# Three edits to a four-layer transformer kernel on one Trainium2 core: first keys loaded during the layer's norm, four of sixteen heads scaled by ScalarE, the norm's root taken on columns and spread by TensorE

## The reference, cut to what matters

```python
x = x + tanh(g_xattn[l]) * xattn_l(layernorm(x), ctx)
x = x + tanh(g_ffn[l])   * ffn_l(layernorm(x))
```

```python
for i in range(6):
    q, k, v = split(shift_tokens(x) @ Wqkv[i])
    q, k = rope(l2norm(q) * qs), rope(l2norm(k) * ks)
    x = local_attention(q, k, v) @ Wo[i] + x
    t = shift_tokens(x)
    xn = (t - mean(t)) / sqrt(var(t) + 1e-5) * g + b
    a, gate = split(xn @ W1 + b1)
    x = (a * gelu(gate)) @ W2 + b2 + x
```

## Time and profile before

| what | value |
|---|---|
| profiled execution | 8037.15 us, span on the core 8035.4 us |
| three other runs | median 8040.48 us (8039.37 to 8040.94) |
| attention, layer 0: norm's first instruction to the first maximum | 160.50 to 207.03 us |
| local transformer, six layers | 5294 to 6711 us, 235.5 us each |
| of these 235.5 us: first rotation to last copied head | 5539.32 to 5614.27 us in the second layer |

### The profile page before, as it was taken

One profiled execution on the slowest core, in us unless ns is written; L12 is line 12 of the kernel. 1 busy time (PEld: TensorE's weight loads), 2 busy tenths in 40 slices (PEclk: granted clock), 3 DMA queues, 4 the chain that ended last, 5 costly groups with the idle time before them and its releaser, 6 DMA issues. The chain is left out here.

```text
span 8035.4 us, 123712 instructions
## 1 busy us (share of the span) xinstructions
PE 5948.6 (74%) x45093; PEld 1946.0 (24%) x45093; DVE 6533.6 (81%) x11562; ACT 5210.8 (65%) x8393; POOL 755.1 (9%) x394
## 2 busy tenths in 40 slices
PE   5699997499997455534555777767888875899987
PEld 2122222122222111101110111134444442222223
DVE  5999972699992899999997999966656665999934
ACT  3399995089997455424545999954555551699992
POOL 2000000000000000000000000054435540000000
PEclk8699999699998555555557999988989996899998
DMA  7100001300000000000002000000000002000001
GB/s 220 40 16 5 18 2 48 73 4 18 17 3 4 22 8 8 13 4 8 8 4 50 17 17 3 1 30 14 9 14 11 9 9 59 3 17 18 3 2 48
DMA packets 112345, 176.36 MB, mean 22 GB/s; under 512 B 14817, under 2 KB 94725, under 8 KB 106750
## 3 DMA queue, kind: packets, MB, share of 16 engines
q1 hardware_dynamic: 111774, 168.91, 8.3%
HBM read 125.66 MB, written 43.21 MB: 21 GB/s over the span
## 5 line engine op out<-in xcount | busy, mean ns | idle before, releaser
L1034 DVE TENSOR_REDUCE a_partial<-a_row 128x2 f32<-128x988 f32 x2496 | 2739.8, 1179 | 130.7 <-PE a_row L908 127.6
L999 ACT ACTIVATE a_prob<-a_score 128x512 f32<-128x512 f32 x4896 | 2649.4, 595 | 110.8 <-PE a_score L921 98.4
L934 PE MATMUL a_acc<-a_prob,a_v_all 128*9 128x256 f32 x19584 | 1526.1, 384 | 0.6 <-ACT a_prob L999 0.6
L517 ACT COPY m_rows<-m_score 128x1536 f32<-128x1536 f32 (+1 forms) x640 | 760.9, 1250 | 847.2 <-DVE m_edge L568 691.4
L908 PE MATMUL a_row<-a_kg,a_qn 54*128 54x494 bf16 x4992 | 1030.9, 410 | 272.1 <-DVE a_partial L1034 212.6
L576 DVE MAX8 m_cand<-m_rows 128x8 f32<-128x192 f32 x4352 | 1213.8, 332 | 13.6 <-ACT m_rows L517 13.6
L496 PE MATMUL m_score<-m_kb,m_qb 54*128 54x512 bf16 (+1 forms) x1664 | 766.3, 608 | 415.3 <-ACT m_rows L517 349.4
L921 PE MATMUL a_score<-a_qb,a_kg 54*128 54x512 bf16 x4896 | 939.4, 380 | 70.8 <-ACT a_prob L999 25.7
L798 DVE SCALAR_TENSOR_TENSOR a_prob<-a_score,a_prob 128x1024 f32<-128x1024 f32 x816 | 925.0, 1216 | 37.9 <-ACT a_prob L774 37.9
L774 ACT ACTIVATE a_prob<-a_score,a_lower 128x1024 f32<-128x1024 f32 x816 | 865.9, 1111 | 84.6 <-PE a_score L715 34.1
L908 PEld LDWEIGHTS a_row<-a_kg,a_qn 54*128 54x128 bf16 x4992 | 243.6, 94 | 1386.8 <-DVE a_partial L1034 1228.9
(11 more groups left out here) (305 smaller groups left out, 5692.5 us busy)
## 6 DMA issues: line engine op xcount, KB each, us to landing
kst<-kv_parts SPq DMA_DIRECT2D x48, 384.0 KB, 3.9
a_kg<-kst SPq DMA_DIRECT2D x60, 306.0 KB
vst<-kv_va SPq DMA_DIRECT2D x48, 288.0 KB, 4.1
e_cb<-comb SPq DMA_DIRECT2D x25, 512.0 KB
a_kg<-kst SPq DMA_DIRECT2D x60, 204.0 KB
a_v_all<-vst SPq DMA_DIRECT2D x3, 3672.0 KB
qst<-q_parts SPq DMA_DIRECT2D x24, 256.0 KB
a_kg<-kst SPq DMA_DIRECT2D x60, 102.0 KB
```

The lines of the kernel that those rows point to most:

```text
L517: act.copy(rows[i][:, c * CH:c * CH + n], score[(i * NCH + c) % 2][:, 0:n]).then_inc(copied, 1)
L934: last = pe.matmul(acc[32 * j:32 * j + VW, columns], v_all[:, k, u // NQC * G + j, :], prob[tile % PROBS][:, j // 2, j % 2, columns], star ...
L999: act.activation(prob[tile % PROBS][:, j // 2, j % 2, :], score[use % 3][:, :], ACT.Exp).then_inc(slot_out, 1)
L1034: dve.tensor_reduce(partial[:, u % 2, 2 * item:2 * item + 2, c], row[use % 2][:, :, 0:CW], AX, ALU.max).then_inc(reduced, 1)
```

## The change

**First keys.** For layers 0, 1 and 3 the stage allocates `first_keys` (which takes the place of the buffer `kg[0]`) and a semaphore `first_loaded`. `norm_transpose` gets a SyncE program that issues the eight DMAs of heads 0 and 1; `attend_with_max` issues only those of heads 2 and 3 at its start.

**Scaling.** GpSimd multiplies heads 0 to 11 (`LP = 12`); ScalarE multiplies heads 12 to 15 by four instructions of 128x64 per step, after the root and before `keep_heads`. The transposes of a step wait for both, and so does VectorE's inversion two steps later.

**Root on columns.** The variance now comes as columns: per half four matmuls with the squares as stationary operand and one column of `mean_ones` as moving operand. Root and reciprocal work on 128x4 values. Four matmuls per half with the broadcast column as stationary operand and the identity as moving operand spread it over all partitions again, and VectorE multiplies by that PSUM tile.

```diff
-def norm_transpose(nc, xs, ident, xT, tag):
+def norm_transpose(nc, xs, ident, xT, tag, first_loads=None):
...
+        if first_loads is not None:
+            @block.sync
+            def _(sp):
+                first_loads(sp)
...
+def load_first_keys(sp, first_keys, first_loaded, kst_l, kmask_l):
+
+    for j in range(2):
+        load_key_rows(sp, first_keys[64 * j:64 * j + ROWS, 0, :], kst_l[j], kmask_l, first_loaded)
...
-            load_keys(0)
+            load_keys(0, range(2, G))
...
             def turn_heads(layer, s):
                 n = layer * STEPS + s
                 pe.wait_ge(S["scaled"], n + 1)
+                pe.wait_ge(S["scaled_act"], n + 1)
...
-                    pe.matmul(bank[2 + half], mean_ones[:, :], f_sq[half], start=True,
-                              stop=True).then_inc(S["var_done"], 1)
+                    for i in range(HALF // P):
+                        last = pe.matmul(bank[4 + half][:, i:i + 1], f_sq[half][:, i * P:(i + 1) * P], mean_ones[:, 0:1],
+                                         start=True, stop=True)
+                    last.then_inc(S["var_done"], 1)
+                for half in range(2):
+                    pe.wait_ge(S["rstd_ready"], layer * 2 + (half + 1))
+                    for i in range(HALF // P):
+                        last = pe.matmul(bank[2 + half][:, i * P:(i + 1) * P],
+                                         rstd_cols[:, half, i:i + 1].to_broadcast([P, P]), ident[:, :], start=True,
+                                         stop=True)
+                    last.then_inc(S["spread"], 1)
...
+            def scale_rest(n):
+                act.wait_ge(S["rn_ready"], n + 1)
+                act.wait_ge(S["added"], n + 1)
+                for h in range(LP, LH):
+                    last = act.activation(t1[n % T1S][:, h, :], t1[n % T1S][:, h, :], ACT.Copy,
+                                          scale=rnorm[:, n % 2, h, :])
+                last.then_inc(S["scaled_act"], 1)
...
-                    act.activation(f_a[half], bank[2 + half], ACT.Sqrt, bias=eps[:, 0:1]).then_inc(S["std_ready"], 1)
+                    act.activation(std_cols[:, half, :], bank[4 + half][:, 0:HALF // P], ACT.Sqrt,
+                                   bias=eps[:, 0:1]).then_inc(S["std_ready"], 1)
...
-                pool.tensor_tensor(t1[n % T1S][:, :, :], t1[n % T1S][:, :, :],
-                                   rnorm[:, n % 2, :, :].to_broadcast([P, LH, LD]), ALU.mult).then_inc(S["scaled"], 1)
+                pool.tensor_tensor(t1[n % T1S][:, 0:LP, :], t1[n % T1S][:, 0:LP, :],
+                                   rnorm[:, n % 2, 0:LP, :].to_broadcast([P, LP, LD]), ALU.mult).then_inc(S["scaled"], 1)
...
-                    dve.reciprocal(f_b[half], f_a[half]).then_inc(S["rstd_ready"], 1)
-                    dve.wait_ge(S["rstd_ready"], layer * 2 + (half + 1))
-                    dve.tensor_tensor(f_x[half], f_r[half], f_b[half], ALU.mult).then_inc(S["xn_mul"], 1)
+                    dve.reciprocal(rstd_cols[:, half, :], std_cols[:, half, :]).then_inc(S["rstd_ready"], 1)
+                for half in range(2):
+                    dve.wait_ge(S["spread"], layer * 2 + (half + 1))
+                    dve.tensor_tensor(f_x[half], f_r[half], bank[2 + half], ALU.mult).then_inc(S["xn_mul"], 1)
```

More of the change, by code:

```diff
@@ L803, in _, with attend_with_max @@
             heads(UNITS - 1)
-def attend_with_max(nc, kst_l, kmask_l, vst_l, qst, ident, att, tag):
+def load_first_keys(sp, first_keys, first_loaded, kst_l, kmask_l):
+    for j in range(2):
+        load_key_rows(sp, first_keys[64 * j:64 * j + ROWS, 0, :], kst_l[j], kmask_l, first_loaded)
+def attend_with_max(nc, first_keys, first_loaded, kst_l, kmask_l, vst_l, qst, ident, att, tag):
     UNITS = NG * NQC
@@ L819, in attend_with_max @@
         m = Memory(nc, ctx, tag)
-        kg = [m.sb(f"kg{i}", [P, 2, KPAD], BF16) for i in range(2)]
+        kg = [first_keys, m.sb("kg1", [P, 2, KPAD], BF16)]
         qn = [m.sb(f"qn{i}", [P, 2, QC], BF16) for i in range(2)]
@@ L833, in attend_with_max @@
         qn_loaded = [m.sem(f"qn_loaded{i}") for i in range(2)]
-        kg_loaded = [[m.sem(f"kg_loaded{i}{pair}") for pair in range(2)] for i in range(2)]
+        kg_loaded = [[first_loaded, m.sem("kg_loaded01")], [m.sem(f"kg_loaded1{pair}") for pair in range(2)]]
         cleared, v_loaded = m.sem("cleared"), m.sem("v_loaded")
@@ L863, in _, with load_keys @@
         def _(sp):
-            def load_keys(g):
-                for j in range(G):
+            def load_keys(g, heads=range(G)):
+                for j in heads:
                     load_key_rows(sp, kg[g % 2][64 * (j % 2):64 * (j % 2) + ROWS, j // 2, :], kst_l[g * G + j], kmask_l,
@@ L1571, in local_transformer @@
     T1S = 4
+    LP = 12
     with ExitStack() as ctx:
@@ L1579, in local_transformer @@
         eps = m.sb("eps", [P, 1])
+        std_cols, rstd_cols = m.sb("std_cols", [P, 2, HALF // P]), m.sb("rstd_cols", [P, 2, HALF // P])
         mean_ones = m.sb("mean_ones", [P, P])
@@ L1600, in local_transformer @@
             "cleared", "setup", "loaded", "wqk", "wvo", "w12", "tables", "shifted",
-            "proj", "squared", "roped", "added", "summed_sq", "root", "inverted", "rn_ready", "scaled", "turned_qk", "kept_qk",
+            "proj", "squared", "roped", "added", "summed_sq", "root", "inverted", "rn_ready", "scaled", "scaled_act", "turned_qk", "kept_qk",
             "v_done", "v_kept", "sc_done", "maxed", "exped", "rs_ready", "rinv_ready", "normed", "turned", "pt_ready",
             "pv_done", "o_ready", "y_done", "z_ready", "mean_done", "xc_ready", "xsq_ready", "var_done", "std_ready",
-            "rstd_ready", "xn_mul", "xn_ready", "h_done", "gelu_ready", "hh_ready", "f_done")}
+            "rstd_ready", "spread", "xn_mul", "xn_ready", "h_done", "gelu_ready", "hh_ready", "f_done")}
         halves = lambda t: [t[:, :, :].rearrange("p h d -> p (h d)")[:, i * HALF:(i + 1) * HALF] for i in range(2)]
@@ L1815, in _ @@
                         root(n - 1)
+                    if 2 <= s < STEPS + 2:
+                        scale_rest(n - 2)
                     if s >= 3:
@@ L1931, in invert @@
                     dve.wait_ge(S["scaled"], n - 1)
+                    dve.wait_ge(S["scaled_act"], n - 1)
                 dve.reciprocal(bounded[:, n % 2, :, 0:1], norm[:, n % 2, :, :]).then_inc(S["inverted"], 1)
@@ L2052, in attention @@
                 top, att = s.sb("top", [P, H * NT]), s.sb("att", [P, NT, D])
-                norm_transpose(nc, xs, ident, xT, f"n{l}")
+                first_loads = None
+                if l != 2:
+                    first_keys = s.sb("first_keys", [P, 2, KPAD], BF16)
+                    first_loaded = s.sem("first_loaded")
+                    first_loads = lambda sp: load_first_keys(sp, first_keys, first_loaded, kst[l], kmask[l])
+                norm_transpose(nc, xs, ident, xT, f"n{l}", first_loads)
                 queries(nc, xT, a[f"wq{l}"], a[f"bq{l}"], float(score_scale[l]), qst, f"q{l}")
@@ L2059, in attention @@
                 else:
-                    attend_with_max(nc, kst[l], kmask[l], vst[l], qst, ident, att, f"a{l}")
+                    attend_with_max(nc, first_keys, first_loaded, kst[l], kmask[l], vst[l], qst, ident, att, f"a{l}")
                 project(nc, att, a[f"wo{l}"], a[f"bo{l}"], a["g_xattn"][l:l + 1], xs, ident, f"p{l}")
```

## The result

The changed kernel takes 7951.4 us (median of 4 runs, 7950.9 to 7955.7), the kernel before beside it 8040.7: ratio 0.9889, interval 0.9875 to 0.9903, 89 us less. The forecast was 7939. The profiled execution took 7955.7 us with a span of 7953.9, the longest of the four. From one attention's norm to the next, the changed kernel's trace is shorter by 10.9, 9.0 and 9.0 us in layers 0, 1 and 3, and by 52.6 us in layer 2, where the local transformer is.

A forecast was written before the change was run, and what follows sets the result against it. Bounds: key waits at attention starts, GpSimd's pace in stage 1 with VectorE close behind, and stage 3's chain at half clock. Gains 27 + 29 + 45 = 101 us from 8037.15 gave 7936, 7939 for the median; range 7908 to 7975.

The forecast's parts named there:

- First keys: Attention start, layers 0, 1, 3: queries 17.3 us earlier less 7.5 for late `q_w`, three times, less clearings: 27 us.
- Root on columns: Stage 3 of the local transformer: third weight block 7.6 us earlier in each of six layers, 45 us.
- The three places: Key waits at attention starts (58.1 us), GpSimd's 4.18 us step in stage 1, stage 3's chain with TensorE's clock at 0.50.
- what is taken off the keys' wait comes off the total: Attention: the 114 maxima behind the wait run back to back on VectorE and need no other late load.
- The rival in which `q_w` passes the keys: Attention start: DMA engines give the small load a turn, nothing is late; 22 us more gained, 7917; chance 0.07.
- The clearings: Three more semaphore clearings with a meeting of all engines, put at 0.7 us each.
- Scaling by ScalarE: Stage 1 of the local transformer: GpSimd's step becomes 3.72, VectorE's 3.85 is next; 4.9 us a layer, 29 in six.
- the 15 steps of 3.84 without a wait: Stage 1: 15 steps of 3.84 and 2.50 from first rotation to first addition reach the last addition 4.4 us earlier.
- This holds if the clock stays up. It should: Stage 3: condition of the 7.6 us a layer, TensorE keeping its full clock; called the least certain term.
- The rival for that case: Stage 3: the clock falls all the same; 2.5 us gained a layer, 15 in six, time 7969; chance 0.27.
- gaps of under 1 us are too short for a fall: Stage 3: the 5.59 us without work shrink to gaps under 1 us filled with small matmuls, so TensorE's clock should stay.
- Slower: Stage 1: ScalarE becomes the bound, deciding at 0.73 us a scaling; at 0.8 the time is about 8080; chance 0.03.

The follow-up runs named there:

- weights_first: Changed kernel with the queries' weight and bias loaded in the norm's block ahead of the key DMAs in layers 0, 1 and 3; 7932.4 us.
- clock_stage3: Changed kernel with filling matmuls on TensorE in stage 3 (12 before the means, 3 behind them, 3 behind the squares' sums); 7947.8 us.
- all_three: Changed kernel with weights ahead of keys (layer 2 too) and filling matmuls at stage 2's end and in stage 3, two more between the sums' halves; 7887.8 us.
- keys_only: Kernel before with only the first head pair's keys loaded from the norm on; 8008.8 us.
- scaling_only: Kernel before with only ScalarE scaling four of sixteen heads; 8019.1 us.
- root_only: Kernel before with only root and reciprocal on columns, spread by TensorE; 7994.6 us.
- pool8: Changed kernel with 8 heads scaled by GpSimd and eight by ScalarE; 7940.1 us.
- pool14: Changed kernel with 14 of 16 heads scaled by GpSimd and two by ScalarE; 7946.6 us.

## Why the prediction was right, and where its sizes were off

*What bounds.* The three places were read rightly: each edit alone gained in its own stage, more than measurement noise. One step did not hold in full, that what is taken off the keys' wait comes off the total: 28.9 of 34.0 us did.

*First keys*, forecast 27 us: measured 29 between the traces, 31 alone. That this is so near is in part two errors that cancel. The gain at the first key product was 11.4, 10.8 and 11.8 us instead of 9.8, since `q_w` lost 6.2, 6.6 and 5.3 instead of 7.5 and the queries arrived 3.0 us after their issue instead of 3.4; against these 4.6 us more than forecast stand the 4.5 lost before the last maxima. The rival in which `q_w` passes the keys is out; what it would have been worth, 19 us measured by weights_first, was there for moving two issues. The clearings: about 1.2 us for 2.

*Scaling by ScalarE*, forecast 29: 25.0. GpSimd's twelve heads took 1.47 us (1.40 forecast), the four scalings 1.06 (1.1), steps 3.85 as forecast. The term that was mis-sized is the 15 steps of 3.84 without a wait, 57.6 us a layer: they took 57.8 to 58.6, since VectorE waits 0.4 to 1.1 us once a layer for squares that are late at a half clock. Over six layers that is the whole 4 us; the end of the stage came as forecast. The wait stood in the trace before, where GpSimd hid it.

*Root on columns*, forecast 45: 36.6. The sentence that failed is "This holds if the clock stays up. It should". It fell in all six layers, while the spread ran or just before the means. The rival for that case had 15 us, and was wrong too: it kept the clock down to the third block, and it was back at 1.00 within the first. The truth lay between, nearer the forecast. The reason given, that gaps of under 1 us are too short for a fall, is what clock_stage3 refutes: it fell in four layers with hardly a gap. With the clock up, all_three gave 43.4 of the 45.

*What the sum lacked*: the tail of stage 2. It was taken as unchanged because its code is. It lost 7.1 us, keys_only and scaling_only lost the same, root_only won 6.2. The sum between the two traces: 101 forecast, less 8 in stage 3, 4 in stage 1, 7 in the tail, 4 from means to root and 2.6 in layer 2's attention, whose code is the old, and 5 and 2 more at projections and keys: 82. The spans differ by 81.5; the medians by 89, since the changed kernel's profiled execution was its longest.

*Slower*: ScalarE's price of a scaling was 0.27, about a third of the 0.73 that it needed, and in pool8 even eight heads only just made it the bound.

## What to carry to other kernels

When loads are moved ahead on a queue, look at what small load is pushed behind them: the order of two issues was worth 19 us, two thirds of the edit itself. Where TensorE's work thins out ahead of a dense stretch, price the clock's fall there as a term of its own, in code that isn't touched as well, for its moment shifts with any edit upstream; filling matmuls in idle time brought the tail from 182.4 to 151.2 us. When the bound of a loop is taken away, look at the waits of the next engine: a wait that was hidden before comes out. Compare small variants only when the clock is held, or else (pool14) a worse one looks even.

## What the runs showed that was not expected

In clock_stage3 TensorE's granted clock fell from 1.00 to 0.52 while it was busy 2.00 of 2.00 us, with matmuls of one column, three of 512 columns and then ones of 128 columns; in two of six layers the same work kept 1.00. The same code, `wo` and the outputs ahead of it, took 25.2, 29.1 or 30.4 us in layers of one and the same kernel (root_only), as its start moved. On ScalarE a 128x64 scaling with a per-partition scale lasts 0.34 us, and each further one in a row adds 0.24. A semaphore's clearing with the meeting of all engines costs 0.39 to 0.45 us.
